# A graph-transformer kernel in which two attention layers' table terms are awaited before a barrier, a logits operand is laid out anew, and the accumulation follows its matmul by one chunk instead of two

## The reference, cut to what matters

```
xl = (x @ W).reshape(n, H, C)
a_src = einsum('nhc,hc->nh', xl, att_src)
a_dst = einsum('nhc,hc->nh', xl, att_dst)
src, dst = edges plus one loop per node
logits = leaky_relu(a_src[src] + a_dst[dst], 0.2)
seg_max = segment_max(logits, dst)
ex = exp(logits - seg_max[dst])
denom = segment_sum(ex, dst)
out = segment_sum(xl[src] * (ex / denom[dst]), dst) + bias
return layernorm(out) * gamma + beta
```

## Time and profile before

| | |
|---|---|
| three runs | 8043.11, 8044.76, 8045.03 us; median 8044.76 |
| the profiled execution | 8043.11 us, span of its trace 8041.4 us |
| mean granted TensorE clock | 0.789 |
| busy | PE 5747.8 us (71%), PEld 3427.9, DVE 4385.0 (55%), ACT 1008.3, POOL 4143.3 (52%) |
| layer 0: source ends, logits, pass | 812.2; 850 to 1104; 1154 to 1699 |
| layer 2: source ends, logits, pass | 4065.2; 4065 to 4371; 4472 to 5073 |

### The profile page before, as it was taken

One profiled execution on the slowest core, in us unless ns is written; L12 is line 12 of the kernel. 1 busy time (PEld: TensorE's weight loads), 2 busy tenths in 40 slices (PEclk: granted clock), 3 DMA queues, 4 the chain that ended last, 5 costly groups with the idle time before them and its releaser, 6 DMA issues. The chain is left out here.

```text
span 8041.4 us, 71776 instructions
## 1 busy us (share of the span) xinstructions
PE 5747.8 (71%) x20790; PEld 3427.9 (43%) x20790; DVE 4385.0 (55%) x10830; ACT 1008.3 (13%) x2591; POOL 4143.3 (52%) x4069
## 2 busy tenths in 40 slices
PE   4766657746767668857686677386778888874886
PEld 3544433325534333335543444263443224333775
DVE  7575357773155545553244877676643884546111
ACT  1211001111110010011100122120010001001221
POOL 1776537733447737714453566106752774772222
PEclk9998557658988866568855899598889997565998
DMA  1100333325533423315532233203333773333454
GB/s 49 43 26 14 94 83 106 106 50 156 157 93 105 103 58 105 105 42 162 139 74 60 82 96 94 49 14 106 102 91 109 210 210 103 105 105 80 160 158 128
DMA packets 355848, 791.05 MB, mean 98 GB/s; under 512 B 96685, under 2 KB 212666, under 8 KB 341298
## 3 DMA queue, kind: packets, MB, share of 16 engines
q0 software_dynamic: 213504, 491.66, 24.2%
q1 hardware_dynamic: 141963, 294.80, 10.8%
HBM read 708.94 MB, written 77.24 MB: 98 GB/s over the span
## 5 line engine op out<-in xcount | busy, mean ns | idle before, releaser
L2095 PE MATMUL bank<-arena 128*125 128x256 f32 (+3 forms) x5824 | 2655.8, 557 | 873.3 <-DMA arena<-TAB,arena 407.0
L2078 POOL DMA_INDIRECT arena<-TAB,arena x2080 | 1982.1, 953 | 1397.3 <-DMA TAB<-arena 761.9
L2095 PEld LDWEIGHTS bank<-arena 128*125 128x125 f32 x5824 | 1126.8, 236 | 2354.6 <-DVE arena L2118 731.2
L2138 DVE TENSOR_TENSOR arena<-bank,arena 125x256 f32 (+3 forms) x2912 | 1359.7, 467 | 1265.5 <-PE bank L2095 1021.9
L2078 POOL DMA_INDIRECT arena<-TABa,arena x832 | 829.6, 997 | 566.8 <-DVEq L138 259.3
L2118 DVE TENSOR_SCALAR arena<-arena 128x125 f32<-128x125 f32 x2080 | 666.2, 321 | 51.0 <-DMA TAB<-arena 35.4
L1306 POOL DMA_INDIRECT SUM<-arena x192 | 307.8, 1603 | 627.0 <-DVE arena L1527 592.1
L1715 POOL DMA_INDIRECT REC<-arena x400 | 471.3, 1178 | 290.0 <-DVE arena L1933 168.4
L1357 PE MATMUL bank<-arena 128*128 128x256 f32 x2048 | 489.0, 395 | 138.3 <-DVE arena L1515 71.3
L1524 DVE TENSOR_TENSOR arena<-bank,arena 128x512 f32<-128x512 f32 x96 | 66.5, 692 | 928.6 <-PE bank L1371 928.6
L297 PE MATMUL bank<-arena 128*125 128x256 f32 (+4 forms) x1600 | 453.9, 432 | 135.0 <-issue 40.8
(11 more groups left out here) (493 smaller groups left out, 5715.0 us busy)
## 6 DMA issues: line engine op xcount, KB each, us to landing
arena<-L_ffn_pack SPq DMA_DIRECT2D x32, 2054.0 KB, 8.2
arena<-L_ffn_pack SPq DMA_DIRECT2D x64, 1026.0 KB, 5.5
arena<-TAB,arena POOLq DMA_INDIRECT x2080, 2.8
arena<-DLR SPq DMA_DIRECT2D x52, 500.0 KB
arena<-SLR SPq DMA_DIRECT2D x31, 500.0 KB
arena<-TABa,arena POOLq DMA_INDIRECT x832, 2.8
TAB<-arena SPq DMA_DIRECT2D x20, 625.0 KB
arena<-L_ffn_b SPq DMA_DIRECT2D x96, 128.0 KB, 5.5
```

The costliest lines, as they stand in the source:

```text
L2078: e.indirect_dma_start(out=m.G[k % RING][:, 0:m.width], out_offset=None, in_=m.table[:, :], in_offset=bass.IndirectOffsetOnAxis(ap=eidx[:, ...
L2095: e.matmul(ps[0:P, 0:m.full], m.S[k % SRING], m.G[k % RING], start=True, stop=True).then_inc(*put("pass_p", m.g, "summed", k))
L2138: e.tensor_tensor(o, banks.of(m.g, "added", k)[0:P, 0:m.full], o, ALU.add).then_inc(*put("pass_v", m.g, "added", k))
```

## The change

Five edits. `pass_dve` adds the result of chunk k - 1 in iteration k for passes with heads too, where it was k - 2. `adx` is laid out as (KC, 2H, 3) instead of (6H, KC): the 6H values of a chunk lie side by side, and a copy of one value for all chunks writes with a step of 6H. `source_sp` waits for the terms to have landed before it goes to the barrier. The terms' transfer counts on the tables' semaphore `gat_t`, and the waits on `table` in `logits_dve`, `rows_sp` and ahead of `pass_pool` are gone. `as3` and `big` take the place of `asT`.

```diff
@@ pass_dve
-        lag = 2 if m.heads else 1
-        for k in range(KC + lag):
+        for k in range(KC + 1):
             upto(k)
             onehot(k + 2)
             if m.heads and k < KC:
                 weigh(k)
-            if k >= lag:
-                add(k - lag)
+            if k:
+                add(k - 1)
@@ Gat
-            self.as3 = [at(44744 + 100 * j, H * T, dt=BF16) for j in range(3)]
-            self.big = at(45044, H * T, p=T, dt=BF16)
-            self.adx = at(B, 6 * H, KC, p=P, dt=BF16)
+            self.as3 = [at(o - 1024 + 100 * j, H * T, dt=BF16) for j in range(3)]
+            self.big = at(o - 724, H * T, p=T, dt=BF16)
+            self.adx = at(B, KC, 2 * H, 3, p=P, dt=BF16)
@@ source_sp
-        e.dma_start(rows(a.terms, P), a.asT).then_inc(*land("gat_u", a.g, "terms"))
+        e.dma_start(rows(a.terms, P), a.asT).then_inc(*land("gat_t", a.g, "terms"))
+        e.wait_ge(*of(a.g, "terms"))
@@ logits_pe
-                                   a.adx[:, :, i * 16 + k], start=True, stop=True)
+                                   a.adx[:, i * 16 + k].rearrange("p j s -> p (j s)"), start=True, stop=True)
@@ logits_act, and the same in logits_dve
-                e.activation(a.adx[:, n, :], banks.of(a.g, "adx", n)[0:P, 0:KC], ACT.Copy).then_inc(
+                e.activation(a.adx[:, :, n // 3, n % 3], banks.of(a.g, "adx", n)[0:P, 0:KC], ACT.Copy).then_inc(
@@ logits_dve, and the same in rows_sp
-        e.wait_ge(*of(a.g, "table"))
@@ gpsimd_program, and the same for gats[1]
-        pass_pool(e, gats[0].run, (gats[0].g, "table"))
+        pass_pool(e, gats[0].run)
```

More of the change, by code:

```diff
@@ L2346, in logits_dve @@
                 e.wait_ge(*of(a.g, "adxmm", n))
-                e.tensor_copy(a.adx[:, n, :], banks.of(a.g, "adx", n)[0:P, 0:KC]).then_inc(
+                e.tensor_copy(a.adx[:, :, n // 3, n % 3], banks.of(a.g, "adx", n)[0:P, 0:KC]).then_inc(
                     *put("logit_v", a.g, "adx", n))
@@ L3065, in gpsimd_program @@
         r = rest(e, r + 1)
-        pass_pool(e, gats[1].run, (gats[1].g, "table"))
+        pass_pool(e, gats[1].run)
         r = rest(e, r + 1)
```

## The result

| | before | after |
|---|---|---|
| median (runs, both on one chip) | 8043.93 us (4) | 8125.15 us (4) |
| lowest, highest | 8041.82, 8045.03 | 8112.95, 8129.58 |
| profiled execution | 8043.11, clock 0.789 | 8120.22, clock 0.791 |

The ratio is 1.0097, 95% interval 1.0081 to 1.0112 (65 to 90 us): slower by 81 us, where +28 was forecast and the range ended at +67.

What follows compares the result with a forecast made beforehand. Stages count singly: source bound by transfers, layer 2's logits by TensorE, layer 0's pass by GpSimd, layer 2's by VectorE. 5.2 + 14.6 - 9.6 - 3 + 1.6 + 0.8 + 0 + 18.5 = +28.1 us: 8073, range 8048 to 8112.

Steps and rivals of the forecast that it cites:

- adx written with a stride: Logits stages: strided copies of adx cost +1.6 us in layer 2 and +0.8 in layer 0, at most +5.7 and +2.9.
- adx read contiguously: Logits stages: ds matmuls read adx faster, -9.6 us in layer 2 and -3 in layer 0; bounds 0 and -15.
- Terms waited for before the barrier: Source stages: everything behind the barrier starts once the terms have landed, +14.6 us in layer 2, +5.2 in layer 0.
- nothing gives it back: Layer 2, behind the source stage: no later work recovers any of the +14.6 us of the wait for the terms.
- Lag 1 instead of 2: Passes: VectorE's add waits for the previous chunk's matmul, 0 us in layer 0 (up to +4), +18.5 in layer 2.
- The price of a place: Layer 2's pass: each of 34 places loses 0.36 us, or about 0.71 with a mix operation beside it.
- exposed in full: Rival, layer 2's pass: all 48 us of lateness count, +58 us in all, 8103 us; chance 0.16.
- Swallowed: Rival, layer 2's pass: VectorE's other idle time absorbs the shorter lag, +10 us in all, 8055 us; chance 0.26.
- The rival of the falling clock: Layer 2's pass: more holes in TensorE's work bring a sixth of it to 1.2 GHz, +45 on top, 8118; chance 0.08.

Runs made afterwards that it cites:

- wide: Kernel before with 24 more copies of adx's banks in layer 0, as fp32 with a 48-byte step into an unread place: 8054.43 us beside 8044.9.
- source: Kernel before with the terms awaited ahead of the barrier, table waits gone, as3 and big moved: 8061.84 us beside 8046.81, ratio 1.0016.

## Why the prediction was wrong

**The step that failed: "adx written with a stride".** It took the fp32 copies of line 2030 as the nearest row and came to +1.6 and +0.8 us, at most +5.7 and +2.9. The copying grew by 31.9 and 14.8 us. The row was right about what it shows: with 4 bytes a value and three times its step, `wide` measured the same 0.85 to 0.89 us. It said nothing of single 2-byte values, 2.3 to 2.5 us. The text named this as what would make it wrong and yet gave it no place in the range: the upper bound came from a row of another width. That this step alone takes the time out of the range is measured: with runs of 4 bytes in the place of single values the changed kernel's two logits stages are 14.0 and 31.2 us shorter, and the kernel has +29.8 us. The step also used the Trainium skill (SBUF: State Buffer, section "Door 1: The DMA port swizzle"): by its note on cachelines each access that crosses to a new 16-byte line pays a penalty. The note gives no price, and that the price is one for both widths was the prediction's own step. The fp32 and the 2-byte copies here touch a new line with every value, and differ by 2.7 times, so counting lines doesn't price them; the measurement decides.

**"adx read contiguously" held.** 0.68 us saved a group in layer 2 (forecast 0.64) and 0.26 in layer 0 (0.32). With runs of 4 bytes, whose copies cost little more than before, the stages gain 1.2 to 4.5 and 8.4 to 10.2 us with the old barrier, and 3.5 and 13.1 with the new one (forecast 3 and 9.6). In the changed kernel layer 2's logits grew by 13.8 less than its copying. Of that 5.2 lie in the groups that are looked up, and 8.3 in the last 12, which took 59.2 us before and 50.9 after. Their ds matmuls, the first and the last rows, and GpSimd's last gather, in order of time, before and then after:

```profile
4310.16 2.83 PE L2315 MATMUL bank<-arena 125*128 125x48 bf16 x32
4321.81 0.94 POOL L2255 DMA_INDIRECT arena<-TERMa,arena  x1 [0.30 <-issue]
4369.32 1.50 PE L2315 MATMUL bank<-arena 125*128 125x48 bf16 x16 [3.13 <-DVE arena L2357]
...
4337.67 0.95 POOL L2255 DMA_INDIRECT arena<-TERMa,arena  x1 [0.30 <-issue]
4365.23 1.46 PE L2315 MATMUL bank<-arena 125*128 125x48 bf16 x32
4416.12 0.82 PE L2315 MATMUL bank<-arena 125*128 125x48 bf16 x16 [3.12 <-DVE arena L2357]
```

Before, the gathers ran on 12.6 us into these groups; after, they had ended 26.6 us ahead of them. That they slow the piece loads there would fit; no run here tests it.

**"Terms waited for before the barrier" held as a mechanism; two sizes were off, and "nothing gives it back" did not hold in the trace of `source` (5.8 us).** Layer 2: 12.7 instead of 14.6. The landing was read from GpSimd's first gather, 3.1 us behind the last byte, and that gather starts 0.73 us after the barrier itself. The transfer rate in 40 slices of 0.55 us, 4073 to 4095 of the changed kernel:

```profile
GB/s 106 108 106 108 106 108 108 108 106 108 106 106 108 108 106 108 109 106 106 106 108 108 62 30 19 18 14 14 13 14 14 13 14 8 1 0 0 0 0 0
```

The last bytes fall in slices 33 and 34, counted from 0 as in the prediction, up to 4091.7 or 4092.2, and the barrier ends at 4093.72: 1.5 to 2.0 us. The figure of the Trainium skill (DMA: Bandwidth & Descriptors, "Anatomy of one DMA"), about 2.0, was the better one; that section is written for transfers that GpSimd issues, and this one is SyncE's. Layer 0: +3.4 instead of +5.2. REC took 5.8 us from issue to use; the forecast had added its 5.2 us of bytes, as they ran in a shared queue, to a fixed part, 7.6 in all. On the empty queue the bytes went faster too, in 3.8 us (827.4 to 831.2).

**"Lag 1 instead of 2": nothing in layer 0 (+1.1 and +2.4, bound 4), too little in layer 2.** The mechanism was right: waits of the add on the pass's matmul behind the mix's matmuls. The price of a place, 0.36 to 0.71 us, was not. It assumed that only the add itself comes out from under the block, at 34 places. But 45 waits are longer than 0.3 us (three were before), and the longest, behind L994, are 2.4 to 4.1 us. In the two places compared, VectorE's hole begins sooner after the start of a block: in the place shown above 4893.80 - 4892.10 = 1.7 us into it, in the earlier trace rows 4781.27 - 4778.92 = 2.35, so there more of the block, and what is queued behind it, is waited out. The pass grew by 29.0 us, 36.8 with the lag alone and 31.4 with the mended layout: between the forecast's 18.5 and the 48 of "exposed in full". Of the 8 us by which it differs from kernel to kernel, some 3 are what this pass moves by in kernels that leave it alone; the rest stays open. "Swallowed" is refuted.

Summed, in the changed kernel: copying +46.7 against +2.4, the lag in layer 2 +29.0 against +18.5, source stages 16.1 against 19.8. The first alone takes the time out of the range.

The rival of the falling clock was summed wrong, though nothing came to hang on it: 70 x (1.23 - 0.6) = 44 us are the pairs alone, and "the mix's as much more" would have to come on top of them. The pass kept its clock of 0.94.

## What to carry to other kernels

Before turning a layout around, look at the narrower side of the write: a single 2-byte value with a step cost 2.7 times a 4-byte one with a step and 4 times a contiguous one, while pairs cost at most 0.17 us a copy more and left the reader what it wanted. If no row has the operation's width, the bound must not come from a row of another width. And taking slack out of a software pipeline on the engine that is the bound cost, here, waits of up to 4.1 us where another engine had a block of work ahead of the hand-over; with blocks half as long the same edit cost 21 us instead of 36. Shorten the blocks first.

## What the runs showed of the hardware

- 416 values from PSUM to SBUF as bf16: 0.52 to 0.59 us contiguous, 0.53 to 0.69 in runs of two, 0.52 to 0.59 in runs of four, 2.27 to 2.48 one by one (5.4 to 6.0 ns a value), with steps of 48 and 96 bytes, on VectorE and ScalarE alike, alone or side by side; back to back they start 1.9 to 2.0 us apart. As fp32 one by one, 48 bytes apart: 0.85 to 0.89.
- TensorE's reading of 48 bf16 columns at a granted clock of 0.50: a step of 832 bytes costs 1.50 us for 16 matmuls, of 8 bytes 0.89, of 4 bytes and of 2 bytes 0.82, so a step of 4 bytes is free here.
- A load of 1248 KB issued on an empty queue was used 5.8 us later.
